# The reload of a span's neighbour lists becomes a counted loop: one turn when no span follows, in place of 49 gathers always

## What is computed

```python
x = _layernorm(x + _L0_gnn_ref(...))                 # two mean convolutions, 128 -> 256 -> 256 -> 128
x = _layernorm(x + _L1_gnn_ref(x, edge_index))       # Moebius: one neighbour after the other
x = _layernorm(x + _L2_gnn_ref(x, node_vec1, ...))   # equivariant messages, segment sums
x = _layernorm(x + _L3_gnn_ref(x, edge_index, ...))  # graph attention, softmax over the neighbours

# _L1: out[dst] is folded with one message after the other, which does not commute
def body(out, em):
    m, idx = em
    return (out.at[idx].set(mobius_add(out[idx], m)), None)
total, _ = jax.lax.scan(body, out0, (messages, dst))
# _L3: alpha = leaky(a_src[src] + a_dst[dst] + a_edge); w = softmax over each dst's edges; out = sum of w * h[src]
```

## Time and profile before

| | us |
|---|---|
| median of 3 runs | 8342.73 |
| lowest and highest of them | 8337.8, 8345.1 |
| span of the profiled execution, first to last instruction | 6643.0 |
| median less that span | 1699.7 |
| POOL busy in the span | 4715.5 (71%) |
| DVE busy in the span | 3828.0 (58%) |

### The profile page before, as it was taken

The page is one execution under the profiler, slowest core; times in us unless marked ns, Lnnn a source line. Parts: engine busy times, 40 slices in busy tenths (PEclk is TensorE's granted clock), DMA queues, the critical chain, the costliest instruction groups (busy, mean ns, idle before and its releaser), DMA issues. The chain is left out here.

```text
span 6643.0 us, 85029 instructions
## 1 busy us (share of the span) xinstructions
PE 2811.4 (42%) x14090; PEld 2095.6 (32%) x14090; DVE 3828.0 (58%) x13952; ACT 1759.4 (26%) x5934; POOL 4715.5 (71%) x4855
## 2 busy tenths in 40 slices
PE   7999899566777670000000026666666400000000
PEld 6777799354555450000000013333334300000000
DVE  4434444665654463667667857777777724434566
ACT  1111000311111010333333247777775000000002
POOL 5777777377777766777777367777777277777766
PEclk7777655788888775555555568888887755555555
DMA  4333333876666632222222124444444332222221
GB/s 110 102 100 99 100 101 101 230 220 198 192 197 194 190 91 59 55 55 55 55 55 55 23 79 105 104 103 103 104 104 121 103 106 56 56 56 56 56 49 56
DMA packets 539521, 672.58 MB, mean 101 GB/s; under 512 B 172996, under 2 KB 403430, under 8 KB 538964
## 3 DMA queue, kind: packets, MB, share of 16 engines
q0 software_dynamic: 187216, 447.02, 25.9%
q1 hardware_dynamic: 256964, 122.61, 7.6%
q10 hardware_dynamic: 95040, 99.62, 4.7%
HBM read 561.52 MB, written 107.30 MB: 101 GB/s over the span
## 5 line engine op out<-in xcount | busy, mean ns | idle before, releaser
L820 POOL DMA_INDIRECT s_rows<-y_split,srcS x880 | 869.8, 988 | 349.3 <-issue 250.4
L1346 POOL DMA_INDIRECT mb_rows<-x_tab,mb_idx x882 | 832.8, 944 | 343.3 <-issue 260.6
L1761 POOL DMA_INDIRECT eq_ring<-fx_tab,srcS x880 | 866.8, 985 | 285.7 <-issue 267.6
L502 POOL DMA_INDIRECT s_rows<-in_x,srcS x880 | 855.2, 972 | 298.1 <-issue 261.9
L2046 POOL DMA_INDIRECT gt_rows<-h_tab,gt_idx x882 | 834.2, 946 | 293.4 <-issue 264.2
L1780 ACT ACTIVATE eq_ring<-eq_ring 128x64 f32<-128x64 f32 x3520 | 863.9, 333 | 310.1 <-DVE eq_ring L1857 268.7
L1798 PE MATMUL eq_ps<-eq_ring,eq_onehot 128*128 128x320 f32 x1760 | 703.5, 557 | 485.3 <-DVE eq_onehot L206 422.8
L1798 PEld LDWEIGHTS eq_ps<-eq_ring,eq_onehot 128*128 128x128 f32 x1760 | 401.0, 238 | 787.2 <-DVE eq_acc L1865 566.0
L1002 DVE TENSOR_TENSOR s_agg<-s_agg,s_ps 128x256 f32 x880 | 370.0, 420 | 450.6 <-PE s_ps L896 311.2
L896 PE MATMUL s_ps<-s_onehot,s_rows 128*128 128x128 bf16 x5280 | 485.2, 249 | 318.5 <-DMA s_rows<-y_split,srcS 280.2
L1455 PE MATMUL mb_ps<-ident,mb_rows 128*128 128x128 f32 x49 | 16.0, 377 | 1382.5 <-ACT mb_rows L1422 1381.4
(11 more groups left out here) (434 smaller groups left out, 5828.9 us busy)
## 6 DMA issues: line engine op xcount, KB each, us to landing
w_tab<-s_wrow ACTq DMA_DIRECT2D x220, 264.0 KB, 2.5
eq_ring<-w_tab SPq DMA_DIRECT2D x880, 66.0 KB
s_es<-in_side ACTq DMA_DIRECT2D x220, 136.0 KB
mb_rows<-x_tab,mb_idx POOLq DMA_INDIRECT x882, 2.5
gt_rows<-h_tab,gt_idx POOLq DMA_INDIRECT x882, 2.5
s_rows<-in_x,srcS POOLq DMA_INDIRECT x880
s_rows<-y_split,srcS POOLq DMA_INDIRECT x880
eq_ring<-fx_tab,srcS POOLq DMA_INDIRECT x880
```

The costliest lines, as they stand in the source:

```text
L502: pool.indirect_dma_start(rows[:, n % SLOTS, :], None, a["x"], bass.IndirectOffsetOnAxis(ap=s["srcS"][:, n:n + 1], axis=0)).then_inc(gathe ...
L820: pool.indirect_dma_start(rows[:, n % SLOTS, :], None, t["ys"], bass.IndirectOffsetOnAxis(ap=s["srcS"][:, n:n + 1], axis=0)).then_inc(gath ...
L1346: pool.indirect_dma_start(rows[:, r, n, :], None, t["x1"], bass.IndirectOffsetOnAxis(ap=idx[:, r, n:n + 1], axis=0)).then_inc(gathered[r][ ...
L1761: pool.indirect_dma_start(frow[:, n % SLOTS, :], None, features, bass.IndirectOffsetOnAxis(ap=s["srcS"][:, n:n + 1], axis=0)).then_inc(gat ...
```

## The change

The reload at the end of a span becomes a loop on POOL (`reload_spans`) whose number of turns is read from the chip. DVE works it out (`plan_next`): 49 if the largest degree is above the new `base`, else 1. Each turn copies one column of list positions to `reload_at` with POOL, waits for the copy, gathers one tile's lists into a buffer `again` of its own, waits for the landing, and copies `again` to the place of the list, again with POOL and a wait. With a span to follow, the same lists are loaded as before; with none, only the first tile's.

```diff
+def plan_next(dve, do, s):
+    q = s["plan_q"]
+    do(dve.tensor_scalar(s["base"][:], s["base"][:], float(SPAN), None, ALU.add))
+    do(dve.tensor_reduce(q[:, 0, 0:1], s["tile_max"][:], AX_X, ALU.max))
+    do(dve.tensor_scalar(q[:, 0, 0:1], q[:, 0, 0:1], s["base"][0:1], float(TILES - 1), ALU.is_gt, ALU.mult))
+    do(dve.tensor_scalar(s["reload"][:], q[:, 0, 0:1], 1.0, None, ALU.add))
+    plan_span(dve, do, s)
+
+def reload_spans(pool, s, into, which, gather, copied, landed, took):
+    count = pool.value_load(s["reload"][0:1, 0:1], min_val=1, max_val=TILES)
+    with pool.Fori(0, count) as n:
+        pool.tensor_copy(s["reload_at"][:], s["span_at"][:, which, bass.ds(n, 1)]).then_inc(copied, 1)
+        pool.wait_ge(copied, 2 * n + 1)
+        pool.sem_inc(took, 1)
+        gather().then_inc(landed, 16)
+        pool.wait_ge(landed, 16 * n + 16)
+        pool.sem_inc(took, 1)
+        pool.tensor_copy(into(n)[0], into(n)[1]).then_inc(copied, 1)
+        pool.wait_ge(copied, 2 * n + 2)
+        pool.sem_inc(took, 1)
...
@@ moebius, per_span; gat likewise
-        per_span = [*idx_ready, gm_ready, copied_ready, multiplied, scaled_ready, folded]
+        per_span = [*idx_ready, gm_ready, copied_ready, multiplied, scaled_ready, folded, r_copied, r_landed]
@@ moebius, POOL; gat likewise with span_edges, edges_in and t["edge"]
-                for n in range(TILES):
-                    span_sources(pool, a, s, n).then_inc(span_in, 16)
-                pool.wait_ge(span_in, c * (16 * TILES) + 16 * TILES)
+                reload_spans(pool, s, lambda n: (s["span_src"][:, bass.ds(n, 1), 0:SPAN].rearrange("p o k -> p (o k)"), again[:]), 0,
+                             lambda: pool.indirect_dma_start(again[:], None, a["src"].rearrange("(e o) -> e o", o=1),
+                                                             bass.IndirectOffsetOnAxis(ap=s["reload_at"][:, 0:1], axis=0)),
+                             r_copied, r_landed, took)
                 pool.sem_inc(src_ready, 1)
@@ moebius, DVE; gat likewise
-                do = Chain(dve, plan_own, c * (PLAN_OPS + 1))
-                do(dve.tensor_scalar(s["base"][:], s["base"][:], float(SPAN), None, ALU.add))
-                plan_span(dve, do, s)
+                do = Chain(dve, plan_own, c * NEXT_OPS)
+                plan_next(dve, do, s)
```

More of the change, by code:

```diff
@@ L162, in build @@
             "plan_i": sb("plan_i", [1, 2, 8], I32),
+            "reload": sb("reload", [1, 1], I32),
+            "reload_at": sb("reload_at", [P, 1], I32),
         }
@@ L1217 @@
 PLAN_OPS = 5 + NG + 6 + (NG - 1) + 4
+def plan_next(dve, do, s):
[5 more added lines that the diff above has]
+    plan_span(dve, do, s)
+NEXT_OPS = 4 + PLAN_OPS
+def reload_spans(pool, s, into, which, gather, copied, landed, took):
[10 more added lines that the diff above has]
+        pool.sem_inc(took, 1)
 def span_sources(pool, a, s, n):
@@ L1288, in moebius @@
         rdeg = sb("rdeg", [P, TILES])
+        again = sb("again", [P, SPAN], I32)
         nodes_in = sem("nodes_in")
@@ L1307, in moebius @@
         own = sem("own")
-        span_in = sem("span_in")
-        per_span = [*idx_ready, gm_ready, copied_ready, multiplied, scaled_ready, folded]
+        r_copied, r_landed = sem("r_copied"), sem("r_landed")
+        per_span = [*idx_ready, gm_ready, copied_ready, multiplied, scaled_ready, folded, r_copied, r_landed]
         block = ctx.enter_context(nc.Block())
@@ L1564, in _ @@
                             turn(p, b, r)
-                do = Chain(dve, plan_own, c * (PLAN_OPS + 1))
-                do(dve.tensor_scalar(s["base"][:], s["base"][:], float(SPAN), None, ALU.add))
-                plan_span(dve, do, s)
-                assert do.n == PLAN_OPS + 1, do.n
+                do = Chain(dve, plan_own, c * NEXT_OPS)
+                plan_next(dve, do, s)
+                assert do.n == NEXT_OPS, do.n
                 dve.sem_inc(arrived, 1)
@@ L1977, in gat @@
         rdeg = sb("rdeg", [P, TILES])
+        again = sb("again", [P, SPAN * EF])
         x_in, w_in, own = sem("x_in"), sem("w_in"), sem("own")
@@ L1984, in gat @@
         last_ready, last_back = sem("last_ready"), sem("last_back")
-        src_ready, span_in = sem("src_ready"), sem("span_in")
+        src_ready, r_copied, r_landed = sem("src_ready"), sem("r_copied"), sem("r_landed")
         arrived, go, took = sem("arrived"), sem("go"), sem("took")
@@ L1989, in gat @@
         consumed = [[sem(f"consumed{r}_{g}") for g in range(NG)] for r in range(2)]
-        per_span = [*idx_ready, below_ready, ex_ready]
+        per_span = [*idx_ready, below_ready, ex_ready, r_copied, r_landed]
         scattered = sem("scattered")
@@ L2051, in _ @@
                 pool.sem_inc(took, 1)
-                for n in range(TILES):
-                    span_edges(pool, t, s, edges_in[:, n * SPAN:(n + 1) * SPAN].rearrange("p k f -> p (k f)"), n).then_inc(span_in, 16)
-                pool.wait_ge(span_in, c * (16 * TILES) + 16 * TILES)
+                reload_spans(pool, s, lambda n: (edges_in[:, bass.ds(n * SPAN, SPAN), :].rearrange("p k f -> p (k f)"), again[:]), 1,
+                             lambda: pool.indirect_dma_start(again[:], None, t["edge"].rearrange("(e o) -> e o", o=1),
+                                                             bass.IndirectOffsetOnAxis(ap=s["reload_at"][:, 0:1], axis=0)),
+                             r_copied, r_landed, took)
                 pool.sem_inc(src_ready, 1)
```

## The result

The changed kernel took 8284.4 us (median of 4, 8277.7 to 8291.5) against 8343.9 for the kernel before (8337.8 to 8349.7). The ratio is 0.9932, with a 95% interval from 0.9918 to 0.9947: 59 us less by the medians, between 44 and 68 by the interval. The forecast was 8320.6, with a range from 8295 to 8336; the direction was right, the size was not.

The account below looks back on a forecast made before the run. POOL was taken to bound the Moebius scatters after an excess reload, and only slightly the kernel's end. 20.5 there plus 1.6 at the end gave 22.1 us: 8342.7 - 22.1 = 8320.6 us, range 8295 to 8336.

Parts of the forecast that it names:

- The reload lies on the path only past 3866.86, and the removal is worth 20.5 in the Moebius layer: Moebius layer: ACT's first group is ready at 3866.86; the last scatter starts at 3929.3 in place of 3949.80, 20.5 us earlier.
- the sum's 3867.95: Moebius layer: predicted start of the first scatter, 3866.86 + 0.25 for POOL to see the counter + 0.85 for the additions.
- The end of the kernel gives 1.6: Scatters to `out`: only the wait past group 6's readiness can be won; 1.8 us earlier, 1.6 after a held step.
- The extra 0.3 for a held step: End of the kernel: DVE's last blocking operation may hold one scatter step by 0.3 us, lowering 1.8 to 1.6.
- The additions cost 0.85 at each place: Both layers: three chained DVE operations (0.7) and two more counters for SP to clear (0.15); bounds 0.6 to 1.1.
- One turn costs nothing: Both reloads: POOL's single turn of 6 to 8 us is hidden, ending before POOL is needed for scatters.
- the rule that whichever of the two engines starts second is fully blocked: Moebius reload: DVE and POOL share a port pair; copies and gather could be held until 3827, the turn ending at 3833.
- port blocking eats part of the gain: Rival, Moebius scatters: four DVE runs hold scatters up to 1.93 us each, 7.7 in all; gain 14.4, time 8328; 13%.
- The count comes out as 49: Rival, both reloads: 49 serial turns take 245 to 390 us in each layer; time near 8700 or above; 2%.
- the turn outlasts its cover: Rival, both reloads: slow POOL copies make a turn outlast its cover; with 100 us at each place, about 8399; 3%.
- What lies around the span I carry over unchanged, since the edit is inside it: Whole kernel: the 22.1 us gain on the span, 6643.0 to 6620.9, was subtracted unchanged from the timed 8342.7.
- the unseen 1699.7 us lie inside: Rival, whole kernel: POOL steps 0.35 longer without profiler, gain 68.9, time 8274; a uniform 1.256 stretch gives 27.8, 8315; 18%.

Follow-up runs that it names:

- e0: The kernel before, unchanged, run once more: 6635.08 us in the traced run, median 6639.3 us.
- e1: Against the kernel before, the change in the Moebius layer only, attention keeping its 49 gathers: 6608.4 us, ratio 0.9956.
- e5: The kernel before, unchanged, run on the same chip as the changed kernel: 6646.7 us.
- e4: The changed kernel, run beside the unchanged kernel before on one chip: 6616.4 us against 6646.7, ratio 0.9954.
- e9: The kernel before, unchanged, on the third chip, run for its trace there: 6637.4 us.
- e8: The changed kernel beside the kernel before on the third chip: 6610.5 us against 6637.4, ratio 0.9960.
- e2: Against the kernel before, the change in the attention layer only, Moebius layer as before: 6633.7 us, ratio 0.9994.
- e6: The changed kernel with the 49 unrolled gathers back in place of the counted loop, so only the additions remain: 6642.3 us, ratio 0.9993 to the kernel before.
- e3: The kernel before with each 49-gather reload cut to one gather, without loop, added DVE operations, copies or counters: 6611.7 us, ratio 0.9961.
- e7: The changed kernel with six reload turns in place of one in both layers: 6621.8 us, ratio 0.9959 to the kernel before.
- the long execution: The changed kernel's own recorded trace, of the slower of two kinds of executions: 8284.8 us, span 8282.7; later the kernel before took about 6640 us.

## Why the prediction was right and where it failed

**The reload lies on the path only past 3866.86, and the removal is worth 20.5 in the Moebius layer: right, with some luck in the size.** Measured on three pairs of traces: 20.6 (e0, e1), 20.7 (e5, e4), 20.2 (e9, e8). Two deviations of about 1 us cancel in it. The trace that the sum was read from has a tail of 155.6, against 154.4 to 154.8 in the three later ones: in it the second gather of the reload was held beside DVE's run, in the others the third (3816.10 in e5), and each gather that passes first saves a step of 1.25. And the first scatter came 72.9 behind the last gather, 0.9 earlier than the sum's 3867.95 makes it.

**The end of the kernel gives 1.6: right in the path, and near in size.** Measured 2.1 (e0, e2), 2.0 (e5, e4) and 2.0 (e9, e8). How much there is to win hangs on two scatters ahead of group 6 that are longer than the usual 0.97 in the kernel before, here in e5 (timeline of POOL):

```profile
6607.27 1.88 POOL L2060 DMA_INDIRECT out<-gt_acc,perm  x1 [0.31 <-issue]
6609.45 1.82 POOL L2060 DMA_INDIRECT out<-gt_acc,perm  x1 [0.30 <-issue]
```

In e1 and e6, which keep the 49 gathers here, only one of the two is long, and their tails are 151.3 and 152.3. So of the 2 us up to 1.5 can also come and go without the removal. In e4 the last 14 scatters start with the readiness of group 6 and run without a gap (timeline of POOL):

```profile
6590.43 1.03 POOL L2095 DMA_INDIRECT out<-gt_acc,perm  x1 [7.10 <-ACT gt_acc L2133]
...
6606.93 1.59 POOL L2095 DMA_INDIRECT out<-gt_acc,perm  x1 [0.31 <-issue]
```

Between 6590.43 and 6606.93 are 13 steps of 1.27, as summed. The extra 0.3 for a held step was not needed.

**The additions cost 0.85 at each place: right for `go` in the Moebius layer, too much elsewhere.** There `go` comes 0.86 later for POOL, but between e3 and e4 only 0.4 of it reaches the first scatter. In attention POOL starts 0.6 later and the first scatter comes 0.5 later. (The sum's list of SP has 37 steps in attention, not 38; that changes nothing.)

**One turn costs nothing: right in the end, wrong in a part.** The copies were to take below 1 us. With one turn they took 0.2 to 0.4, but for the second copy of the Moebius turn: 7.5 to 8.2 us in six traces, one of them with six turns, and in e1 it was the gather that took 12.06. The prediction took the earlier trace rows to agree with the rule that whichever of the two engines starts second is fully blocked. They agree only in part: the gather at 3813.91 lies within the run of 49 too and took 0.94, and so do the copy at 3820.09 and the gather at 3821.21 in e4, with 0.31 and 1.04. In each trace but that of e3, whose one gather passed, one POOL operation, started 1.7 to 5.6 us into the run, stood until the run was over, and the one or two ahead of it passed. What picks it was not found: the gathers of e1 and e4 both start 1.74 into the run. On the timeline of DVE in e4, that run:

```profile
3819.48 12.95 DVE L1611 SCALAR_TENSOR_TENSOR mb_fold<-mb_xd,mb_cz,mb_fold 128x128 f32<-128x128 f32 x49 [1.02 <-SPq L1360]
```

The copy that started at 3824.77 ended at 3832.55, 0.1 behind the run. With 37 to 40 us of cover left it changed nothing.

**Left out of the sum: about 2 us.** The barrier behind the Moebius layer is 12.6 from the last scatter to the next gather's start, in place of 13.8 (e4, e5), and from the last scatter to the end of the kernel 13.4 in place of 14.2. Both follow the number of gathers in their own layer's reload, whatever else the kernel has: 12.6 and 13.4 in every trace with one gather (e3 has none of the additions), 13.0 and 13.8 with six (e7), 13.8 and 14.2 with 49 (e2 in the Moebius layer, e1 in attention, e6 in both). Why was not tried. Tails, barrier and end together are 24.8 us (e5 to e4) and 24.1 (e9 to e8), against 22.1 forecast and 30, 27 and 24 timed; the stages that the edit does not touch differ from trace to trace by up to 12 us either way (the stretch up to the first Moebius gather 2611 to 2622, the equivariant gathers 1136 to 1144), enough for the rest.

**The rival "port blocking eats part of the gain" fell**: the 48 scatter steps took 61.16 in place of 61.38. **"The count comes out as 49" and "the turn outlasts its cover" fell**, by one turn and 37 us of slack.

**The step that failed is "What lies around the span I carry over unchanged, since the edit is inside it".** Almost nothing lies around it: every later time is its span and about 2 us, and so is the recorded one of the changed kernel (8284.8 and 8282.7). The 1699.7 us were inside the timed executions, as the rival "the unseen 1699.7 us lie inside" said, to which I gave 18%; for the kernel before that is inferred, since no span of its long executions is on record. But the mechanism of that rival was wrong as well: in the long execution POOL's step is 1.25 to 1.27 as ever, and neither its 68.9 nor the 27.8 of a uniform stretch is the 59 measured. What is longer is other engines' time between instructions. Of the 1662 us between the spans of the long execution and of e4, 518 lie ahead of the first Moebius gather, 524 in the Moebius rounds, 396 in the equivariant gathers, 217 between these and the last attention gather, and 7 in the Moebius tail. The waits of the changed kernel (total us, times, longest us), first in the long execution, then in e8 ("remote" is a wait whose end the profile can put down to nothing on this core):

```profile
ACT mb_ps L1416 <- remote: 725.0, 45, 22.5
PEld s_ps L898 <- issue: 630.2, 601, 16.3
DVE mb_prod L1532 <- issue: 377.2, 346, 4.1
DVE mb_dots L1532 <- issue: 164.3, 157, 2.5
DVE mb_q L1532 <- issue: 158.5, 170, 1.8
DVE mb_prod L1532 <- ACT mb_ps L1416: 83.2, 7, 65.1
```

```profile
ACT mb_ps L1416 <- DMA mb_rows<-x_tab,mb_idx: 548.7, 66, 54.1
DVE mb_prod L1532 <- ACT mb_ps L1416: 291.0, 75, 9.1
DVE mb_prod L1532 <- issue: 78.0, 6, 60.9
PEld s_ps L898 <- issue: 68.0, 112, 2.8
```

DVE stops 346 times ahead of `mb_prod` for nothing that the profile shows, 1.1 us on average, and 6 times in the other kind. With the stops ahead of `mb_dots` and `mb_q` that is 700 us in the rounds in place of 78, while its waits for ACT there fall from 291 to 83. Two such stops, on the timeline of DVE in the long execution; the durations of 0.08 and 0.29 are those of e8 for the same forms of operation:

```profile
4703.30 0.08 DVE L1532 DVE_READ_ACCUMULATOR2_ANT mb_dots<- 128x1 f32 x1 [0.34 <-issue]
...
4704.72 0.29 DVE L1532 CUSTOM_DVE_ANT_0 mb_prod<-mb_ps,mb_fold 128x128 f32<-128x128 f32 x1 [0.60 <-issue]
```

The Moebius rounds take 1701 us in place of 1175, the equivariant gathers 1534 in place of 1139, while the attention tail is 150.9 in place of 150.8. What puts an execution in this kind was not found.

**What stays open is why 59 and not 25.** The Moebius tail of the changed kernel is 141.4 in the long execution, 7 more than elsewhere, and the time to its first scatter is 72.9 as ever. If the tail before was POOL-bound there as here, near 155, the two tails and the barriers give about 17 us. That 155 is an estimate; no trace shows it. The remaining 42, at least 27 by the interval, would lie in stages that the edit does not touch. Each kernel's four times lie within 14 us, so it is no scatter from one execution to the next. Whether it is the change's, or something else that differed between the two sets of executions, could be told only by a trace of the kernel before of the long kind. The four occasions of the experiments did not give one. Nor do e3 and e6 rule out there what they rule out in the short kind, that the shape or the addresses of the program matter: no run of the long kind tried it. So the failed step says why a sum read from a short execution could not be laid on the long times; where the 42 come from it does not say, and their cause is not known.

## What to carry to other kernels

Work at the end of a stage is worth only what reaches past the next thing that its engine is needed for: 60 us of gathers removed gave 20 to 21 where POOL was the bound behind them, and at most 2 where the finishing engines were. A loop with a count from the chip lets general code skip its general case, but its serial turn (4.4 us here against 1.25 for an unrolled gather) is a price if the general case ever comes. And when the trace's span and the timed median differ by a quarter, that is the first thing to explain: compare like with like before summing anything, and don't forecast finer than that difference allows.

## What the runs showed of the hardware

Beside an unbroken run of 49 DVE operations with two inputs on chip (12.95 us, one every 0.26) one POOL operation stood until the run was over: a gather (12.03 in the kernel before, 10.72 in e5, 12.06 in e1, in place of 0.94 to 1.04), or a copy of 48 columns (7.78 in e4, in place of 0.22 to 0.33). The held gathers ended 0.8 to 0.9 us behind the run, the copies 0.1. One or two POOL operations ahead of it, within the same run, took their usual time. Which one is held differs between runs whose Moebius layer is the same (e1 and e4).

The same instructions can take 25% longer in all, with the same durations on DVE (0.29 and 0.08 for the four forms of L1532) and POOL (0.95 a gather). In the long execution DVE stopped between instructions of the Moebius rounds for 0.2 to 4.1 us, 1.1 on average ahead of `mb_prod`, and TensorE and ACT for longer; POOL's steps did not change.
